# Score buffers filled by halves in two int8 attentions, and three unused products in the first one's steps without a projection

## The reference, cut to what matters

```python
def _attn(x, ctx, wq, wk, wv, wo, bo, dq, dk, dv, dw):
    ...
    sim = jnp.einsum('bhid,bhjd->bhij', _fq(q, dq, 128.0, 8), _fq(k, dk, 128.0, 8)) * SCALE
    attn = jax.nn.softmax(sim, axis=-1)
    out = jnp.einsum('bhij,bhjd->bhid', _fq(attn, dw, 0.0, 8), _fq(v, dv, 128.0, 8))
    ...
h1 = _ln(x, ln1_g, ln1_b)
x = _attn(h1, h1, a1_wq, a1_wk, a1_wv, a1_wo, a1_bo, d_q1, d_k1, d_v1, d_w1) + x
h2 = _ln(x, ln2_g, ln2_b)
x = _attn(h2, context, a2_wq, a2_wk, a2_wv, a2_wo, a2_bo, d_q2, d_k2, d_v2, d_w2) + x
```

## Time and profile before

| what | value |
|---|---|
| median of three runs | 1049.2 us (1048.2 to 1049.9) |
| profiled execution | 1049.15 us |
| its span | 1047.4 us |
| TensorE, VectorE, ScalarE, GpSimd busy | 867.2, 763.5, 612.3, 519.7 us |
| TensorE's mean granted clock | 0.862 of full speed |
| first int8 attention, from its first scores | about 22 to 228 us |
| second int8 attention | about 230 to 338 us |

### The profile page before, as it was taken

How to read it: one execution, slowest core, us unless ns; L and a number is a source line. 1 busy time by engine, 2 the same in 40 slices (tenths; PEclk the granted TensorE clock), 3 DMA queues, 4 the chain that set the end, 5 groups by cost and what they waited for, 6 DMA issues and landing times.

```text
span 1047.4 us, 23536 instructions
## 1 busy us (share of the span) xinstructions
PE 867.2 (83%) x8314; PEld 528.5 (50%) x8314; DVE 763.5 (73%) x1680; ACT 612.3 (58%) x1487; POOL 519.7 (50%) x1045
## 2 busy tenths in 40 slices
PE   3798888974555877998999799998988788888895
PEld 1344444442333554555765456565555466565664
DVE  5788888978775664565567667677477788989886
ACT  0777777858885313544355456654555566666674
POOL 2677777776563323763444465655244222333313
PEclk9995555555555989999999899999999999999998
DMA  8400000000000000000000010000000000000000
GB/s 266 150 1 2 0 0 1 1 2 0 1 2 0 2 0 1 2 2 2 1 2 2 20 27 22 25 23 15 2 2 2 1 1 2 2 12 0 10 2 21
DMA packets 23573, 16.39 MB, mean 16 GB/s; under 512 B 8744, under 2 KB 20400, under 8 KB 23344
## 3 DMA queue, kind: packets, MB, share of 16 engines
q1 hardware_dynamic: 23472, 15.06, 5.0%
HBM read 10.85 MB, written 1.05 MB: 11 GB/s over the span
## 4 chain that ended last, share of the span: by engine, by line
PE 49%; DVE 25%; ACT 9%; issue 9%; POOL 6%; DMA 1%; DVEq 1%; SPq 0%; ACTq 0%; POOLq 0%
ACT sb_E L1239 5%; PE ps_context L780 5%; DVE sb_neg_raw L1536 3%; PE ps_context L783 3%; POOL sb_E L2261 3%; PE ps_scores L856 3%; DVE sb_E L1964 3%; PE ps_scores L880 3%; DVE sb_inv_den L1779 2%; PE ps_scores L733 2%; PE ps_scores L773 2%; PE ps_turned L1084 2%; PE ps_scores L674 2%; DVE sb_neg_half L1747 2%; PE ps_turned L694 2%
## 5 line engine op out<-in xcount | busy, mean ns | idle before, releaser
L1239 ACT ACTIVATE sb_E<-ps_scores,sb_neg_max,sb_score_scale 128x256 f32<-128x256 f32 (+1 forms) x384 | 190.9, 515 | 64.0 <-DVE sb_neg_max L1539 63.6
L2261 POOL TENSOR_SCALAR sb_E<-sb_E,sb_inv_sum 128x256 f16<-128x256 f32 x256 | 123.6, 483 | 47.3 <-DVE sb_inv_sum L1576 29.5
L1490 ACT ACTIVATE sb_E<-ps_scores,sb_ff_bias 128x512 f32<-128x512 f32 x128 | 87.6, 688 | 66.6 <-PE ps_scores L1125 64.4
L1142 PE MATMUL ps_turned<-sb_moe_down,sb_E 128*128 128x128 f16 x512 | 92.6, 220 | 23.9 <-DVE sb_E L1964 23.8
L1964 DVE TENSOR_TENSOR sb_E<-sb_E 128x512 f16<-128x512 f32 x128 | 93.1, 745 | 23.4 <-ACT sb_E L1493 21.2
L1536 DVE TENSOR_REDUCE sb_neg_raw<-ps_scores 128x4 f32<-128x1024 f32 (+1 forms) x80 | 97.4, 1218 | 14.4 <-PE ps_scores L674 12.0
L1747 DVE TENSOR_REDUCE sb_neg_half<-ps_scores 128x16 f32<-128x1024 f32 x48 | 58.7, 1223 | 67.1 <-PE ps_scores L856 67.1
L1559 DVE TENSOR_REDUCE sb_neg_quad<-ps_scores 128x2 f32<-128x512 f32 (+1 forms) x96 | 64.5, 685 | 42.2 <-PE ps_scores L735 30.1
L1144 PE MATMUL ps_turned<-sb_moe_down,sb_E 128*128 128x128 f16 x512 | 92.1, 219 | 0.0
L1143 PE MATMUL ps_turned<-sb_moe_down,sb_E 128*128 128x128 f16 x512 | 92.1, 219 | 0.0
L2196 POOL TENSOR_SCALAR sb_veps<-sb_mv 128x2 f32<-128x2 f32 x72 | 17.3, 240 | 148.2 <-DVE sb_mv L1519 144.4
(11 more groups left out here) (285 smaller groups left out, 2257.2 us busy)
## 6 DMA issues: line engine op xcount, KB each, us to landing
sb_moe_up<-in_moe_up SPq DMA_DIRECT2D x1, 2048.0 KB
sb_KS<-sb_qk_parts SPq DMA_DIRECT2D x96, 16.0 KB, 1.8
sb_QS<-sb_qk_parts SPq DMA_DIRECT2D x96, 16.0 KB, 1.8
sb_rows<-in_rows SPq DMA_DIRECT2D x1, 1216.0 KB, 7.5
out_x<-sb_raw_context SPq DMA_DIRECT2D x8, 128.0 KB, 1.8
sb_X<-in_x SPq DMA_DIRECT2D x1, 768.0 KB, 9.5
sb_square<-in_square SPq DMA_DIRECT2D x1, 768.0 KB, 11.0
sb_ctxT<-in_ctxT SPq DMA_DIRECT2D x1, 512.0 KB, 11.2
```

The lines of the kernel that those rows point to most:

```text
L1142: pe.matmul(dst, u_hi, hi, start=(first and i == 0), stop=False, skip_group_check=True)
L1239: last = act.activation(E[:, ring, head], SC[t % 2][:, head], ACT.Exp, bias=neg_max[:, ring, h:h + 1], scale=scale, accum_out=row_sum[:, r ...
L1490: last = act.activation(U_full[:, k % 4, :], banks[k % 4], ACT.Gelu, bias=bias, scale=1 / WEIGHT_SCALE)
L2261: last = pool.tensor_scalar(E16[:, ring, SEQ * h:SEQ * h + SEQ], E[:, ring, SEQ * h:SEQ * h + SEQ], inv_sum[:, ring, h:h + 1], HALF, ALU.m ...
```

## The change

On TensorE, the wait ahead of a unit's scores is split. The first product waits for a new semaphore, `exped_half`, that ScalarE raises when the exponentials of the buffer's first half are done: after the second of four in `a1`, after the eighth (the last out of PSUM) in `a2`. The second product waits for what frees the other half: in `a1` for `exped`, as both did before, in `a2` for `subbed`.

A new function `keep_clock` issues three products of the 128 x 128 f16 identity with a 512-column view of itself into `TP[t % 2]`, where the step's transposes are written right after. It waits for nothing and nobody reads what it writes. It runs after the scores in each step of TensorE's list for the int8 attentions that has no projection: steps 1 to 4 of each eight in `a1`, the two groups of eight before its first unit and the last four such steps of its run-out among them. `a2` has no such step.

```diff
--- before.py
+++ after.py
@@ -303,7 +303,7 @@
     c = dict(round_done=layer.total[0], round_free=layer.total[0], part=layer.total[1],
              bn=NBATCH, stats=NBATCH, eps_added=NBATCH, rstd=NBATCH, z=NBATCH, x_based=NBATCH, context_out=NBATCH)
     c.update(scored=n, maxed=n, exped=n, raw_sum=n // 2, summed=n // 2, normed=n, turned=n, landed=n, valued=n,
-             keyed=NBATCH, raw_max=n)
+             keyed=NBATCH, raw_max=n, exped_half=n)
     if not layer.over_self:
         c.update(subbed=n, row_summed=n // 2, rounded=n, q_cast=NBATCH, v_cast=NBATCH)
     return c
@@ -660,7 +660,7 @@
                 n, u, b = L.steps * p + t, t % L.per_batch, t // L.per_batch % 2
                 if not live(n, L.units):
                     return
-                wait(pe, S["exped"], B["exped"] + n - 1)
+                wait(pe, S["exped_half"], B["exped_half"] + n - 1)
                 if u == 0:
                     wait(pe, S["round_free"], B["round_free"] + L.rounds_before(p, t))
                     wait(pe, S["keyed"], B["keyed"] + L.batch(p, t, "M") + 1)
@@ -671,11 +671,15 @@
                 if L.over_self:
                     group = slice(32 * (u % 4), 32 * (u % 4) + 32)
                     for h in (0, 512):
+                        if h:
+                            wait(pe, S["exped"], B["exped"] + n - 1)
                         last = pe.matmul(dst[:, h:h + 512], QS[group, b, 0, tile:tile + P], KBD[group, b, h:h + 512],
                                          start=True, stop=True)
                 else:
                     for g in range(2):
                         group = slice(64 * g, 64 * g + 64)
+                        if g:
+                            wait(pe, S["subbed"], B["subbed"] + n - 1)
                         last = pe.matmul(dst[:, 512 * g:512 * g + 512], QS[group, b, 0, tile:tile + P],
                                          KBD[group, b, 0:8 * CTX], start=True, stop=True)
                 last.then_inc(S["scored"], 1)
@@ -693,6 +697,12 @@
                 for k in range(8):
                     last = pe.transpose(dst[:, P * k:P * k + P], E16[:, ring, P * k:P * k + P], ident16[:, :])
                 last.then_inc(S["turned"], 1)
+
+            def keep_clock(t):
+
+                for i in range(3):
+                    pe.matmul(TP[t % 2][:, :], ident16[:, :], ident16[:, None, :].to_broadcast([P, 4, P]), start=True,
+                              stop=True)
 
             def quant_values(L, B, p, t):
 
@@ -1034,6 +1044,8 @@
                 quant_scores(L, B, p, t)
                 if n_rounds > 0:
                     round_of(L, B, p, t, 0)
+                else:
+                    keep_clock(t)
                 quant_turn(L, B, p, t)
                 quant_values(L, B, p, t)
                 if n_rounds > 1:
@@ -1239,6 +1251,8 @@
                     last = act.activation(E[:, ring, head], SC[t % 2][:, head], ACT.Exp,
                                           bias=neg_max[:, ring, h:h + 1], scale=scale,
                                           accum_out=row_sum[:, ring, h:h + 1])
+                    if h == (1 if L.over_self else BIASED - 1):
+                        last.then_inc(S["exped_half"], 1)
                 if not L.over_self:
                     act.wait_ge(S["subbed"], B["subbed"] + n + 1)
                     rest = E[:, ring, CTX * BIASED:]
```

## The result

The changed kernel takes 1059.19 us (median of four runs, 1057.46 to 1060.35) against 1048.7 us for the kernel before on the same chips; the ratio is 1.0097, 95% interval 1.0080 to 1.0114. It is slower by 1%, not faster by 0.5%.

What follows compares the result with a forecast made beforehand. In the first attention TensorE at half clock and VectorE were nearly full, the limit changing by step. Periods -5.6, halves -3, start +2 and end +1 us gave -5.6 us: 1043.6 us, forecast 1044, range 1030 to 1083.

Steps and rivals of the forecast that it cites:

- I expect a rise in most periods within step 1 or 2: First attention: added products lift TensorE's clock through about step 5 of each eight; -0.7 us a period, -5.6 us; chance 0.42.
- The two outcomes: Whole kernel: faster by more than 2 us, chance 0.45, or slower, chance 0.43.
- Half clock: First attention, clock not rising: products cost 1.29 us a step, less idle time, +3.7 us a period; no-rise case 1082 us, 0.28.
- With a rise: First attention, period in which the clock rises: score product, turn and projection run faster, -0.7 us a period.
- rises in some periods only: Rival for the first attention: the clock rises in only part of the periods; about +11 us, 1060 us, chance 0.15.
- Halves in the first attention: Split score wait lets one product start earlier; -3 us, between 0 and 9 us; nothing if TensorE has no idle time.
- Halves in the second attention: Split score wait there changes neither wait that holds the scores; worth 0, at most 0.6 us.
- Start: Products ahead of the first attention's first scores delay them; +2 us taken.
- the upper bound of +3.5 us: Delay of the first scores if the 24 products before them run at half clock, scores near 26 us.
- End: Four groups of products while the second attention begins: +2.9 us at half clock, about 0 at full; +1 us taken.
- The rule on transposes: The skill's claim that transposes do not count as busy for TensorE's clock; by it alone the products would raise it.
- 153 to 156 us: Stretch of the first attention before the change: TensorE busy 3.00 of 3 us with turns and scores, clock still at half.

Runs made afterwards that it cites:

- experiment 2: The kernel before with the three added products and its old, unsplit waits: 1060.97 us, ratio 1.0080.
- Experiments 4: The changed kernel with three products in each of the eight steps of the first attention: 1049.35 us, ratio 0.9992.
- 7: The changed kernel with four products in each of the eight steps of the first attention: 1048.93 us, ratio 0.9993.
- 8: The changed kernel with six products behind the projection in step 0 and three in each other step of the first attention: 1049.05 us, ratio 1.0013.
- experiment 9: The changed kernel, its start kept, with four products in each of the first attention's eight steps while units are live, none in the run-out: 1042.45 us, ratio 0.9944.
- experiment 3: The changed kernel with the three products taken over 32 rows of the identity instead of 128: 1061.17 us, ratio 1.0094.
- experiment 6: The changed kernel with twelve transposes of the identity in place of the three products: 1061.29 us, ratio 1.0114.

## Why the prediction was wrong

**The step that failed** is "I expect a rise in most periods within step 1 or 2", and the reason given for it, that the added products fill the gaps with ordinary products on 128 rows. In the profiled run, of the five steady periods two had a rise and three had none, and each rise came within 4 us of the start of a projection, as before the change. From 46 to 104 us TensorE stood at half clock, busy 27.8 of 29 us in each period, and from 76 to 93 us it had no gap at all. So a TensorE without gaps and with these products in its steps was not enough. What the products did in the steady steps is to hold the clock once it was up, for 13 to 14 us instead of 3 to 4. They can stand at a rise as well: the dense ones of the start brought one, and experiment 2 had one in its third step of products, one of the six rises in the steady periods of these two profiles. Experiments 4, 7 and 8 show that more of them lengthen the high stretches but leave the moment of the rise open. With four in every step the profiles show nearly the whole attention at full clock (experiments 7 and 9), and with the start kept early it is faster than before (experiment 9).

**The two outcomes were nearly a toss-up in the prediction**, faster 0.45 and slower 0.43, and the measured time lies inside its wide range only because the range held both.

**The costs of both kinds of period were right.** Half clock: forecast +3.7 us, measured 29.13 to 29.40 against 25.4 to 25.6, +3.7 on average; a step of 3.56 us, measured 3.55. The 1.29 us for three products is twice the 0.65 us at full clock, not the pair of scores scaled up (3 x 0.48 = 1.44); measured 1.25. With a rise: forecast -0.7 for the products alone, measured 24.84 us in experiment 2, -0.7. With the split waits, worth another 0.4 us a period by the forecast, it was 24.79 and 25.42 us, -0.8 and -0.1, less than the two together. The case "rises in some periods only", given 0.15 and 1060 us, is what happened, as these sizes give it: three times +3.7, two times about -0.5, and the rest at the ends. The prediction gives its +11 us for that case without a sum, so that it came near is in part luck.

**Halves in the first attention.** Forecast -3 us, measured -3.5 us at the second attention's first scores and 0.46% in all. That it would be nothing where TensorE has no idle time is borne out: periods at half clock last 29.1 to 29.2 us with the old waits (experiment 2) and 29.1 to 29.4 with the split ones. **Halves in the second attention:** forecast nothing, measured 107.1 against 107.2 us.

**Start.** Forecast +2 us, measured -1.0 us (21.61 against 22.57). The loss that the upper bound of +3.5 us stands for is real, and larger: with products that did not raise the clock (experiment 3) it was +5.3 us. I had not counted that the first projection would halve. The -1.0 us is one profile's: over the seven other profiles with 24 products at the start, or transposes in their place, the first scores came from 21.79 to 23.26 us, against 22.57 and 22.88 without products. **End.** From the last steady projection to the second attention's first scores it took 56.7 us (183.80 to 240.49) against 55.2, +1.5 with a last period partly in it; forecast +1.

**The rule on transposes**, which I said 153 to 156 us agreed with, does not hold here: experiment 6. What sets that stretch apart is then not the transposes; that its scores use 32 rows only, and that experiment 3's 32-row products held nothing up, fits, but no run replaced the scores by full-height ones, so this is argued and not shown.

**Left open:** what decides which projection brings the rise. The last 8 us of TensorE's work ahead of the projection do not decide it alone: the same instructions at the same distances had a rise at one projection and none at another. The periods with a rise were the same in two kernels with the same timing and others where the timing differed; no run moved the moment alone.

## What to carry to other kernels

Work added to lift TensorE's clock is paid at half clock first: count it against TensorE's idle time in a step at half clock, and ask separately what will raise the clock and what will only keep it. Put it where the engine waits anyway, and enough of it that the clock never falls, or leave it out; between the two, some periods pay and few gain. Compare it with the rest of the change alone: here even products that kept the clock up gained nothing that can be told from the split waits alone, until they stood at the end of the step. A change of two parts wants two runs: here one part was worth -0.5% and the other +1%.

## What the runs showed of the hardware

- Full-height f16 transposes held the granted clock up exactly as products did (experiment 6: 0.78 and 0.77 in the same two periods), and 48 of them alone brought it up at the start (first projections 1.13 us). The Trainium skill, "TensorE: Matmul & The Clock Gate", Part 4, says the opposite; the measurement decides.
- 12 dense 128x512 products from 9.5 us had the clock up by the first projection (1.13 us against 2.07); 24 of 32 rows did not, and cost 5.3 us (experiment 3, first projections 2.08 us).
- 17 us of TensorE without a gap, projection and full-height products in it, passed at half clock (76 to 93 us), and the same 11 us of instructions around a projection had a rise once and none another time.
- The page's clock stands at 1.00 until the first recorded change, whatever the clock: before, a pair of scores at 55.78 us lasts 1.03 us, as at half clock, while the page says 1.00.
